# Moving a reciprocal, an attention product and gate injections between the steps of a fused recurrent kernel

## The chip, the cores and the metric

One core of a Trainium2 chip. The time is device time in microseconds (us) of one execution of the whole kernel, from a median of a few runs. A profile of one execution gives a span (first to last instruction) and a trace of every instruction with its start, its duration and what released it. Engines are called PE (TensorE; its weight loads are listed apart as PEld), DVE (VectorE), ACT (ScalarE), POOL (GpSimd) and SP (SyncE).

## The reference, cut to what matters

x is (2, 1024, 256): 2 sequences of 1024 time steps, width D = 256, and there is one condition vector for each sequence. Four residual layers follow one another; the first three work on each time step alone, the last is a recurrence over time.

```python
x = x + attention(x, cond)       # 2 keys only (a fixed one, and one from cond), 16 heads, then W_proj
x = x + experts(x, cond)         # shared gated unit + top 2 of 8 experts, gates s_i / (sum of the top 2 + 1e-9)
x = x + u(cond) @ W_u + x @ W_e  # condition and stream, added
# LSTM over the 1024 steps, h of width 256, 2 sequences:
z = x_t @ Wx + b + h @ Wh;  i, f, o, g = split(z)
c = sigmoid(f) * c + sigmoid(i) * tanh(g);  h = sigmoid(o) * tanh(c)
x = x + hs
```

## The kernel before, in words

The LSTM is a chain of T = 1024 dependent steps, so the kernel is one loop of BATCHES = 128 iterations of U = 8 steps (u = 0 to 7). In the gaps of these steps the engines make the first three layers for the batch of 8 time steps that comes next (NB = 16 rows, 8 steps x 2 sequences). Each engine runs its own loop in the order in which it is written, and the engines meet only in semaphores that count steps; `now` is the count that belongs to the step.

**One step.** PE waits for `hid` (the h of the step before) and runs `recur` (L881 to L888) for the gates f, g and i, then o: weight loads from the ring `h_ring`, matmuls with `wh_sb`, 64 records of each, all at line L885. Then DVE transposes f (L676), g and i (L678) and o (L684) in PSUM, ACT takes tanh of them (L510, L513, L516), DVE forms c with one scan (L686), ACT takes its tanh (L519), DVE writes h (L702) and signals `hid`. What DVE does besides stands at the head of a step (L655 to L674, ahead of its first transpose) or in the slot between the scan and h (L688 to L700). What PE does besides stands after the four `recur` of a step (L902 to L935).

**The side work of one batch, by step.**
- u = 0: PE multiplies the stream by `we_sb` (`stream_mm`), the condition (`cond_mm`) and the shared unit (`down_mm(0)`) into `partial_b`, in bank 7. `stream_made` is signalled after `stream_mm`.
- u = 1: DVE forms x + attention (`attended`, L587) from `attn_b` and `x_a`; PE makes the scores and the routing logits (L738 to L750); ACT takes tanh of the logits (`fall`, L467) and of the scores.
- From there POOL runs `gates` (L364 to L418), one chain of small operations on (128 x 8) or (128 x 64), which asks DVE for three reciprocals: `ratio` (L577, in the slot of u = 2), `s_all` (L581, slot of u = 3) and `inv` (L585, slot of u = 5), the inverse of `den_eps` (L400). After it come `pad` (L353), a copy of the layer's output, and `weigh` (L424, `hid_e`).
- u = 2: PE `down_mm(1)` and `(2)`; u = 3: PE `sum_mm` (L780) gives `x3_b` in bank 7; u = 4: DVE `layer3` copies it to `x3` (L604); u = 4 and 5: PE `up_mm` (L754); u = 5: ACT `unit_acts` (L471, L472); u = 6 slot and head of u = 7: DVE `hidden_a` (L593) and `hidden_s` (L598); head of u = 0: DVE `turn(0)`, the transpose of `hid_s` (L601).
- u = 6: PE `inject_fo` twice (L792): the x-part of f and of o for the next 8 steps is put into their banks. u = 7: PE `inject_gi` (L792, after waits for `padded_out` and `t_gi`) the same for i and g, and then `attend` (L742), attention's product for a later batch, into `attn_b` in bank 5.
- POOL, after the last h of a batch: `half_h` (L452), `y_sb` (L457) and `move` (L429); `h_read` after the first lets DVE overwrite the ring (waited for in the slot of u = 0, L690).

The injected f and o stand in their bank with an offset (`fo = (u + U - FO_AT - 1) % U * B`) since they are made one step ahead of the batch's end; i and g use `u * B`.

PE's loop is written `nc.Fori(..., head_slot={PE_ENGINE: 0})`: the loop's first instruction is loaded at slot 0 of a fetch block, and the code ahead jumps over the padding.

Of the kernel before, what the change touches and what calls it, by code (L numbers as in the profile page):

```python
# [11 lines left out]
P = 128  # L12
# [11 lines left out]
U = 8  # L24
# [17 lines left out]
FO_AT = 6  # L42
# [21 lines left out]
def cond_stack_kernel(nc, x, small, wkv, wq, wproj, up, we, down, wproj2, wu, wx, wh, bias_z, y):  # L64
    ctx = ExitStack()
    with ctx:
# [260 lines left out]
        def _(pool):  # L327
# [36 lines left out]
            def gates(count):  # L364
# [19 lines left out]
                pool.tensor_tensor(lead[:, :, :], rivals, own_sel, ALU.subtract).then_inc(gate_step, 1)  # L384
                pool.wait_ge(gate_step, 7)
# [76 lines left out]
        def _(act):  # L462
# [42 lines left out]
            with act.Fori(READY, READY + T, U) as t:  # L505
                for u in range(U):
                    now = act.snap(t + (u + 1))
                    fo = (u + U - FO_AT - 1) % U * B
                    act.wait_ge(t_f, now)
                    nc.scalar.activation(f_act[:, :].rearrange("p (c b) -> p c b", b=B),  # L510
                                         t_f_b[:, :, fo:fo + B], ACT.Tanh).then_inc(a_f, 1)
                    act.wait_ge(t_gi, now)
                    nc.scalar.activation(gi_out.rearrange("p g (c b) -> p g c b", b=B),  # L513
                                         t_gi_b[:, :, :, u * B:(u + 1) * B], ACT.Tanh).then_inc(terms_in, 1)
                    act.wait_ge(t_o, now)
                    nc.scalar.activation(o_act[:, :].rearrange("p (c b) -> p c b", b=B),  # L516
                                         t_o_b[:, :, fo:fo + B], ACT.Tanh)
# [13 lines left out]
        def _(dve):  # L531
# [55 lines left out]
            def attended(src):  # L587
                nc.vector.tensor_tensor(x1[:, :, :, 0:NB], attn_b.unsqueeze(2).to_broadcast([P, C, J, NB]),
                                        src.unsqueeze(2).to_broadcast([P, C, J, NB]), ALU.add).then_inc(x1_out, U)
# [6 lines left out]
            def hidden_s(count, up_to):  # L596
                dve.wait_ge(hid_a_out, count)
                nc.vector.tensor_tensor(hid_s[:, :], hid_a[:, :], units[:, P:2 * P], ALU.mult).then_inc(hid_s_out, up_to)  # L598
# [17 lines left out]
            attended(x_first[:, 0, :, :])  # L616
# [5 lines left out]
            hidden_s(U, U)  # L622
# [10 lines left out]
            attended(x_first[:, 1, :, :])  # L633
# [10 lines left out]
            hidden_s(2 * U, 2 * U)  # L644
            dve.wait_ge(x3_made, READY)
            layer3(READY)
            dve.wait_ge(w_in["wh"], 16)
# [6 lines left out]
            with dve.Fori(READY, READY + T, U) as t:  # L654
                for u in range(U):  # L655
                    now = dve.snap(t + (u + 1))
                    if u == 0:
                        dve.wait_ge(hid_s_out, now)
                        turn(0, hid_s[:, :], hid_st, U)
                    elif u == 1:  # L660
                        dve.wait_ge(x_ready, now)
                        dve.wait_ge(stream_made, now)
                        attended(x_a[:, :, :])
# [9 lines left out]
                    elif u == 7:  # L673
                        hidden_s(now, U)  # L674
# [22 lines left out]
                    elif u == 5:  # L697
                        invert_inv(now)
                    elif u == 6:
                        hidden_a(now)  # L700
                    dve.wait_ge(cell_tanh, now)
# [6 lines left out]
        def _(pe):  # L708
# [31 lines left out]
            def attend():  # L740
                for c in range(C):
                    last = nc.tensor.matmul(attn_b[:, c, :], value_w[:, c * P:(c + 1) * P], w1_own[:, :],  # L742
# [20 lines left out]
            def stream_mm(up_to):  # L763
                for c in range(C):
                    last = tile_mm(c, x1[:, c, 0, 0:NB], we_sb[:, c, :], True)
                last.then_inc(stream_made, up_to)
# [11 lines left out]
            def sum_mm(up_to):  # L778
# [3 lines left out]
                last.then_inc(x3_made, up_to)  # L782
# [14 lines left out]
            BEHIND = (FO_AT + 1) * B  # L797

            def inject_fo(z, g):
                return inject(z, g, NB, x3[:, :, BEHIND:BEHIND + NB], ones[:, 16:32], True)  # L800
# [21 lines left out]
            attend().then_inc(attn_made, 1)  # L822
# [9 lines left out]
            stream_mm(READY)  # L832
# [6 lines left out]
            pe.wait_ge(own_first, 2)  # L839
            pe.wait_ge(hid_s_out, U)  # L840
            attend().then_inc(attn_made, 1)
            pe.wait_ge(x1_out, 2 * U)
# [19 lines left out]
            pe.wait_ge(own_first, 3)  # L862
# [168 lines left out]
```

## Time and profile before

| | |
|---|---|
| time, median of 3 runs | 2413.18 us (2410.02 to 2414.47) |
| the profiled execution: its time | 2409.16 us |
| the profiled execution: its span | 2407.4 us |
| PE, PEld, DVE, ACT, POOL busy | 85%, 63%, 59%, 36%, 49% of the span |
| chain that ended last, by engine | PE 37%, POOL 22%, DVE 20%, issue 12%, ACT 9% |

Times of rows are us from the span's start. A row of the timeline gives start, duration, engine, line, operation, what is written and read, how many instructions are merged (x64), and in brackets the idle time of that engine just before and what released it. Matmuls are pipelined and their ends are modelled. "issue" is idle time for which the profile shows no releaser. A row of 64 weight loads at L885 is the `recur` of one step; the width of its weights (128x8 and so on) tells the step.

### The profile page before, as it was taken

To read this page: it belongs to the slowest core of one execution; us is meant where nothing else is said; L and a number is where in the kernel's file an instruction comes from. 1 tells how busy PE (TensorE), PEld (TensorE's weight loads), DVE (VectorE), ACT (ScalarE), POOL (GpSimd) and SP (SyncE) were. 2 spreads that over 40 slices of the span, in tenths; PEclk is the share of its full clock that TensorE was granted. 3 is DMA by queue.
4 is the path that set the end of the run, shared out by engine and by line. 5 is a ranking of instruction groups with operands and counts; after the bars stand their busy time and mean duration, and the time that the engine had idled before them with its cause. 6 is when DMAs were issued, how large, how long until landed. Compare 5 with 4: busy or idle time off the path is not lost.

```text
span 2407.4 us, 200920 instructions
## 1 busy us (share of the span) xinstructions
PE 2051.9 (85%) x86306; PEld 1505.9 (63%) x86306; DVE 1420.3 (59%) x7602; ACT 876.7 (36%) x4761; POOL 1169.1 (49%) x5082
## 2 busy tenths in 40 slices
PE   6888888888888888888888888888888888888888
PEld 4666666666666666666666666666666666666666
DVE  2565665566566556656655665665566566556655
ACT  1333333333333333333333333333333333333333
POOL 3445445444544554454455445445544544544454
PEclk8999999999999999999999999999999999999999
DMA  3000000000000000000000000000000000000000
GB/s 135 4 3 2 3 3 2 2 3 3 2 3 3 2 2 3 3 2 3 3 2 2 3 3 2 3 3 2 2 3 3 2 3 3 2 2 3 3 2 3
DMA packets 57581, 14.54 MB, mean 6 GB/s; under 512 B 56161, under 2 KB 56161, under 8 KB 57058
## 3 DMA queue, kind: packets, MB, share of 16 engines
q1 hardware_dynamic: 57570, 14.39, 2.6%
q8 instruction: 8, 0.13, 0.0%
q14 instruction: 3, 0.02, 0.0%
HBM read 12.26 MB, written 2.10 MB: 6 GB/s over the span
## 4 chain that ended last, share of the span: by engine, by line
PE 37%; POOL 22%; DVE 20%; issue 12%; ACT 9%; DVEq 0%; POOLq 0%; ACTq 0%
PE bank L885 28%; DVE bank L678 9%; ACT terms L513 5%; DVE bank L686 5%; PE bank L792 5%; DVE h_ring L702 4%; ACT bank L519 4%; PE bank L742 3%; POOL beats L386 2%; POOL ties L387 2%; POOL ties L389 2%; POOL beats L391 2%; POOL lead L384 2%; POOL beats L358 1%; POOL top L394 1%
## 5 line engine op out<-in xcount | busy, mean ns | idle before, releaser
L885 PEld LDWEIGHTS bank<-wh_sb,h_ring 128*4 128x4 f32 (+2 forms) x65536 | 922.9, 94 | 705.9 <-DVE h_ring L702 700.1
L885 PE MATMUL bank<-wh_sb,h_ring 128*4 128x64 f32 (+2 forms) x65536 | 1107.9, 219 | 296.8 <-DVE h_ring L702 229.7
L510 ACT ACTIVATE f_act<-bank 128x4 f32<-128x4 f32 x1024 | 177.3, 173 | 1026.0 <-DVE bank L676 1026.0
L676 DVE STREAM_TRANSPOSE bank<-bank 128x64 f32<-128x64 f32 x1024 | 271.6, 265 | 390.7 <-PE bank L885 390.7
L678 DVE STREAM_TRANSPOSE bank<-bank 128x64 f32<-128x64 f32 x1024 | 271.5, 265 | 186.1 <-PE bank L885 186.1
L513 ACT ACTIVATE terms<-bank 128x8 f32<-128x8 f32 x1024 | 189.5, 185 | 280.3 <-DVE bank L678 280.3
L372 POOL TENSOR_TENSOR num<-one,fall 128x8 f32<-128x8 f32 x130 | 26.0, 200 | 532.1 <-ACT fall L467 532.1
L754 PE MATMUL bank<-up_sb,x 128*32 128x512 f32 x2080 | 274.0, 599 | 0.7 <-ACT fall L467 0.7
L684 DVE STREAM_TRANSPOSE bank<-bank 128x64 f32<-128x64 f32 x1024 | 271.6, 265 | 0.1
L760 PE MATMUL bank<-down_e,hid_t 128*16 128x256 f32 x3096 | 266.6, 380 | 0.0
L702 DVE SCALAR_TENSOR_TENSOR h_ring<-o_act,bank 128x4 f32<-128x4 f32 x1024 | 161.0, 157 | 138.6 <-ACT bank L519 95.0
L686 DVE TENSOR_TENSOR_SCAN bank<-terms 128x16 f32<-128x16 f32 x1024 | 205.6, 201 | 27.8
L516 ACT ACTIVATE o_act<-bank 128x4 f32<-128x4 f32 x1024 | 177.3, 173 | 39.6 <-DVE bank L684 0.2
L519 ACT ACTIVATE bank<-bank 128x4 f32<-128x4 f32 x1024 | 161.8, 158 | 56.5
L792 PE MATMUL bank<-bias_sb,small_sb 128*16 128x64 f32 (+1 forms) x4128 | 159.2, 219 | 0.0
L681 DVE SCALAR_TENSOR_TENSOR terms<-f_act,bank 128x4 f32<-128x4 f32 x1024 | 152.6, 149 | 0.0
L760 PEld LDWEIGHTS bank<-down_e,hid_t 128*16 128x16 f32 x3096 | 100.9, 97 | 51.8
L792 PE MATMUL bank<-wx_sb,padded 128*32 128x64 f32 (+1 forms) x4128 | 99.0, 221 | 32.9 <-DVE bank L678 32.6
L378 POOL TENSOR_TENSOR num<-num 128x8 f32<-128x8 f32 x520 | 103.8, 200 | 40.8
L585 DVE RECIPROCAL inv<-den_eps 128x1 f32<-128x1 f32 x130 | 21.3, 164 | 158.6 <-POOL den_eps L400 158.6
L792 PE MATMUL bank<-wx_sb,x 128*16 128x64 f32 x4128 | 106.1, 220 | 8.1 <-POOL wx_sb L440 1.5
L792 PEld LDWEIGHTS bank<-wx_sb,padded 128*32 128x32 f32 (+1 forms) x4128 | 78.8, 103 | 53.2 <-issue 53.2
(133 smaller groups left out, 2654.2 us busy)
## 6 DMA issues: line engine op xcount, KB each, us to landing
x_a<-in_x SPq DMA_DIRECT2D x129, 16.0 KB, 1.7
x_s<-in_x SPq DMA_DIRECT2D x129, 16.0 KB, 1.7
up_sb<-in_up SPq DMA_DIRECT2D x1, 2048.0 KB, 8.7
out_y<-y_sb SPq DMA_DIRECT2D x128, 16.0 KB, 1.4
down_sb<-in_down SPq DMA_DIRECT2D x1, 1536.0 KB, 12.5
wx_sb<-in_wx SPq DMA_DIRECT2D x1, 1024.0 KB, 14.2
wh_sb<-in_wh SPq DMA_DIRECT2D x1, 1024.0 KB, 16.3
wkv_sb<-in_wkv SPq DMA_DIRECT2D x1, 512.0 KB, 3.9
```

The costliest lines, as they stand in the source:

```text
L510: nc.scalar.activation(f_act[:, :].rearrange("p (c b) -> p c b", b=B), t_f_b[:, :, fo:fo + B], ACT.Tanh).then_inc(a_f, 1)
L513: nc.scalar.activation(gi_out.rearrange("p g (c b) -> p g c b", b=B), t_gi_b[:, :, :, u * B:(u + 1) * B], ACT.Tanh).then_inc(terms_in, 1)
L519: nc.scalar.activation(c_tanh, cell_c, ACT.Tanh).then_inc(cell_tanh, 1)
L676: nc.vector.transpose(bank[3][:, 0:HC], z_f_b[:, 0:HC]).then_inc(t_f, 1)
L678: nc.vector.transpose(bank[4][:, 0:HC], z_gi_b[:, 0:HC]).then_inc(t_gi, 1)
L684: nc.vector.transpose(bank[3][:, HC:2 * HC], z_o_b[:, 0:HC]).then_inc(t_o, 1)
L686: nc.vector.tensor_tensor_scan(cell_all, factor, addend, 0.0, ALU.mult, ALU.add).then_inc(cell, 1)
L702: nc.vector.scalar_tensor_tensor(out=h_ring[:, u, :, WIN - B:WIN], in0=o_act[:, :].rearrange("p (c b) -> p c b", b=B), scalar=1.0, in1=c_t ...
L754: last = nc.tensor.matmul(units[32 * j:32 * (j + 1), :], x1[:, c, 0, :], up_sb[:, c, j, :], start=(c == 0), stop=(c == C - 1), skip_group_ ...
L760: return nc.tensor.matmul(partial_b[32 * j:32 * j + NB, :], lhs, rhs, start=first, stop=False, skip_group_check=True)
L792: last = nc.tensor.matmul(z[32 * j:32 * j + rows, 0:HC], src[:, c, :] if c < C else const, wx_v[:, c, g, j, :] if c < C else bias_v[:, g, ...
L885: last = nc.tensor.matmul(z[32 * j:32 * j + row + B, 0:HC], h_ring[:, prev, c, WIN - B - row:WIN], wh_v[:, c, g, j, :], start=False, stop= ...
```

## The change

- `invert_inv` (the reciprocal `inv`) goes from DVE's slot of u = 5 to the head of u = 7, behind `hidden_s`.
- DVE's `turn(0)` goes from the head of u = 0 to the slot of u = 7.
- PE's `inject_gi` goes from u = 7 to u = 6, and both `inject_fo` from u = 6 to u = 7; the offsets of the two pairs are exchanged.
- PE's `attend` goes from u = 7 to u = 3, behind `sum_mm`; its target moves from bank 5 to bank 7. `x3_made` is signalled behind it, `stream_made` behind `down_mm(0)`.
- POOL's `pad` goes from behind `gates` into it, behind `lead` (L384), and copies the rows with the offset.
- PE's loop has no `head_slot`.
- Ahead of the loops: waits and the two first `attend` change accordingly, and `turn(0)` runs once more.

```diff
-FO_AT = 6
+GI_AT = 6
-        attn_b = bank[5][:, 64:64 + C * NB].rearrange("p (c t) -> p c t", c=C)
+        attn_b = bank[7][:, D + C * NB:D + 2 * C * NB].rearrange("p (c t) -> p c t", c=C)
+        attn_first_b = bank[6][:, C * NB:2 * C * NB].rearrange("p (c t) -> p c t", c=C)
...
+            BEHIND = (GI_AT + 1) * B
             def pad(count):
                 pool.wait_ge(x3_out, count)
-                return pool.tensor_copy(padded[:, :, NB:2 * NB], x3[:, :, NB:2 * NB])
+                return pool.tensor_copy(padded[:, :, NB:2 * NB], x3[:, :, BEHIND:BEHIND + NB])
...
                 pool.tensor_tensor(lead[:, :, :], rivals, own_sel, ALU.subtract).then_inc(gate_step, 1)
+                if between:
+                    between()
                 pool.wait_ge(gate_step, 7)
...
-                gates(i * U + (READY + U))
-                pad(i * U + (READY + U)).then_inc(padded_out, U)
+                gates(i * U + (READY + U), lambda: pad(i * U + (READY + U)).then_inc(padded_out, U))
...
-                    if u == 0:
-                        dve.wait_ge(hid_s_out, now)
-                        turn(0, hid_s[:, :], hid_st, U)
-                    elif u == 1:
+                    if u == 1:
...
                     elif u == 7:
-                        hidden_s(now, U)
+                        hidden_s(now)
+                        invert_inv(now)
...
-                    elif u == 5:
-                        invert_inv(now)
                     elif u == 6:
                         hidden_a(now)
+                    elif u == 7:
+                        dve.wait_ge(hid_s_out, now)
+                        turn(0, hid_s[:, :], hid_st, U)
                     dve.wait_ge(cell_tanh, now)
...
-            with nc.Fori(READY, READY + T, U, engines=(PE_ENGINE,), head_slot={PE_ENGINE: 0}) as t:
+            with nc.Fori(READY, READY + T, U, engines=(PE_ENGINE,)) as t:
...
-                    recur(z_f_b, GF, fo, prev).then_inc(z_f, 1)
-                    recur(z_gi_b, GC, u * B, prev)
-                    recur(z_gi_b, GI, 16 + u * B, prev).then_inc(z_gi, 1)
-                    recur(z_o_b, GO, fo, prev).then_inc(z_o, 1)
+                    recur(z_f_b, GF, u * B, prev).then_inc(z_f, 1)
+                    recur(z_gi_b, GC, gi, prev)
+                    recur(z_gi_b, GI, 16 + gi, prev).then_inc(z_gi, 1)
+                    recur(z_o_b, GO, u * B, prev).then_inc(z_o, 1)
                     if u == 0:
                         pe.wait_ge(hid_st, now)
-                        stream_mm(U)
+                        stream_mm()
                         cond_mm()
-                        down_mm(0)
+                        down_mm(0).then_inc(stream_made, U)
...
                     elif u == 3:
                         pe.wait_ge(partial_out, now)
-                        sum_mm(U)
+                        sum_mm()
+                        pe.wait_ge(own_out, now)
+                        attend(attn_b).then_inc(x3_made, U)
...
                     elif u == 6:
+                        pe.wait_ge(padded_out, now)
+                        pe.wait_ge(t_gi, now)
+                        inject_gi()
+                    elif u == 7:
                         pe.wait_ge(t_f, now)
                         inject_fo(z_f_b, GF)
                         pe.wait_ge(t_o, now)
                         inject_fo(z_o_b, GO)
-                    elif u == 7:
-                        pe.wait_ge(padded_out, now)
-                        pe.wait_ge(t_gi, now)
-                        inject_gi()
-                        pe.wait_ge(own_out, now)
-                        attend()
```

## Rows read from the trace of the kernel before

**Rows 1.** The page, part 4: the chain that ended last, by engine.
```profile
PE 37%; POOL 22%; DVE 20%; issue 12%; ACT 9%; DVEq 0%; POOLq 0%; ACTq 0%
```

**Rows 2.** Timeline of one iteration, `recur` of u = 2, 4 to 7, 0, 1, 2.
```profile
1200.37 0.90 PEld L885 LDWEIGHTS bank<-wh_sb,h_ring 128*8 128x8 f32 x64 [0.23 <-DVE h_ring L702]
...
1204.53 0.91 PEld L885 LDWEIGHTS bank<-wh_sb,h_ring 128*12 128x12 f32 x64 [0.55 <-DVE h_ring L702]
...
1206.61 0.91 PEld L885 LDWEIGHTS bank<-wh_sb,h_ring 128*14 128x14 f32 x64 [1.05 <-DVE h_ring L702]
...
1209.70 0.91 PEld L885 LDWEIGHTS bank<-wh_sb,h_ring 128*16 128x16 f32 x64 [2.05 <-DVE h_ring L702]
...
1211.78 0.89 PEld L885 LDWEIGHTS bank<-wh_sb,h_ring 128*2 128x2 f32 x64 [0.25 <-DVE h_ring L702]
...
1214.46 0.89 PEld L885 LDWEIGHTS bank<-wh_sb,h_ring 128*4 128x4 f32 x64
...
1216.61 0.90 PEld L885 LDWEIGHTS bank<-wh_sb,h_ring 128*6 128x6 f32 x64 [0.71 <-DVE h_ring L702]
...
1218.69 0.90 PEld L885 LDWEIGHTS bank<-wh_sb,h_ring 128*8 128x8 f32 x64 [0.23 <-DVE h_ring L702]
```

**Rows 3.** Timeline of u = 5, and the waits: us in total, times, longest.
```profile
1209.10 0.22 POOL L400 TENSOR_SCALAR den_eps<-den 128x1 f32<-128x1 f32 x1 [0.16 <-POOL den L362]
...
1209.42 0.16 DVE L585 RECIPROCAL inv<-den_eps 128x1 f32<-128x1 f32 x1 [1.16 <-POOL den_eps L400]
...
DVE inv L585 <- POOL den_eps L400: 158.6, 130, 5.2
```

**Rows 4.** Timeline of u = 7: injection and attention's product.
```profile
1212.70 0.27 DVE L678 STREAM_TRANSPOSE bank<-bank 128x64 f32<-128x64 f32 x1 [0.18 <-PE bank L885]
...
1213.08 0.30 PEld L792 LDWEIGHTS bank<-wx_sb,padded 128*32 128x32 f32 x16 [0.41 <-issue]
...
1213.92 0.52 PEld L742 LDWEIGHTS bank<-w_own,value_w 128*128 128x128 f32 x4
```

**Rows 5.** Timeline of u = 6: the last weight loads of `inject_fo` for o.
```profile
1211.35 0.17 PEld L792 LDWEIGHTS bank<-bias_sb,small_sb 128*16 128x16 f32 x8
```

**Rows 6.** Timeline of u = 3 and the head of u = 4.
```profile
1203.46 0.52 PEld L780 LDWEIGHTS bank<-small_sb,partial 128*128 128x128 f32 x4
...
1204.51 0.19 DVE L604 COPY x<-bank 128x32 f32<-128x32 f32 x1
...
1205.01 0.27 DVE L676 STREAM_TRANSPOSE bank<-bank 128x64 f32<-128x64 f32 x1 [0.31 <-PE bank L885]
```

**Rows 7.** Timeline of DVE, head of u = 7.
```profile
1211.73 0.29 DVE L598 TENSOR_TENSOR hid_s<-hid_a,bank 128x128 f32<-128x128 f32 x1
```

**Rows 8.** Timeline of POOL: `lead`, the first operation behind `inv`, `weigh`, `half_h`.
```profile
1204.54 0.29 POOL L384 TENSOR_TENSOR lead<-sel 128x64 f32<-128x64 f32 x1
...
1210.29 0.20 POOL L411 TENSOR_TENSOR comb<-s_top,inv 128x8 f32<-128x8 f32 x1
...
1212.22 0.61 POOL L424 TENSOR_TENSOR hid_e<-gelu_act,gate_w 128x256 f32<-128x256 f32 x1
...
1213.94 0.24 POOL L452 TENSOR_TENSOR half_h<-h_ring,half 128x32 f32<-128x32 f32 x1 [1.11 <-DVE h_ring L702]
```

**Rows 9.** Timeline of DVE: a transpose in the slot of u = 1; h of u = 0.
```profile
1199.84 0.29 DVE L601 STREAM_TRANSPOSE hid_t<-hid_e 128x128 f32<-128x128 f32 x1
...
1216.40 0.16 DVE L702 SCALAR_TENSOR_TENSOR h_ring<-o_act,bank 128x4 f32<-128x4 f32 x1 [0.29 <-ACT bank L519]
```

**Rows 10.** Timeline of DVE: its first instruction after the loop's back edge.
```profile
1214.09 0.31 DVE L601 STREAM_TRANSPOSE hid_t<-hid_s 128x128 f32<-128x128 f32 x1 [0.29 <-issue]
```

**Rows 11.** Timeline of PE: first `recur` in the loop, and the same of pass two.
```profile
58.80 1.08 PE L885 MATMUL bank<-wh_sb,h_ring 128*4 128x64 f32 x64 [2.11 <-issue]
...
78.62 1.08 PE L885 MATMUL bank<-wh_sb,h_ring 128*4 128x64 f32 x64
```

**Rows 12.** The page, part 3: DMA of instructions, whole run: packets, MB, share.
```profile
q8 instruction: 8, 0.13, 0.0%
```

More of the change, by code:

```diff
@@ L615, in _ @@
             dve.wait_ge(attn_made, 1)
-            attended(x_first[:, 0, :, :])
+            attended(attn_first_b, x_first[:, 0, :, :])
             mask_first(1)
@@ L621, in _ @@
             hidden_a(U)
-            hidden_s(U, U)
+            hidden_s(U)
             dve.wait_ge(hid_s_out, U)
@@ L632, in _ @@
             dve.wait_ge(attn_made, 2)
-            attended(x_first[:, 1, :, :])
+            attended(attn_first_b, x_first[:, 1, :, :])
             mask_first(2)
@@ L738, in scores, with attend @@
                     nc.tensor.matmul(scores_b, score_w[:, c, :], x_s[:, c, :], start=(c == 0), stop=(c == C - 1))
-            def attend():
+            def attend(attn):
                 for c in range(C):
-                    last = nc.tensor.matmul(attn_b[:, c, :], value_w[:, c * P:(c + 1) * P], w1_own[:, :],
+                    last = nc.tensor.matmul(attn[:, c, :], value_w[:, c * P:(c + 1) * P], w1_own[:, :],
                                             start=True, stop=True)
@@ L761, in tile_mm, with stream_mm @@
                                         skip_group_check=True)
-            def stream_mm(up_to):
+            def stream_mm():
                 for c in range(C):
                     last = tile_mm(c, x1[:, c, 0, 0:NB], we_sb[:, c, :], True)
-                last.then_inc(stream_made, up_to)
+                return last
             def cond_mm():
@@ L776, in down_mm, with sum_mm @@
                 return last
-            def sum_mm(up_to):
+            def sum_mm():
                 for c in range(C):
@@ L781, in sum_mm @@
                                             start=True, stop=True)
[L782 removed]
+                return last
             wh_v = wh_sb[:, :, :].rearrange("p c (g j m) -> p c g j m", g=4, j=J)
@@ L821, in _ @@
             pe.wait_ge(own_first, 1)
-            attend().then_inc(attn_made, 1)
+            attend(attn_first_b).then_inc(attn_made, 1)
             pe.wait_ge(value_out, 3)
@@ L831, in _ @@
             pe.wait_ge(we_ident, C)
-            stream_mm(READY)
+            stream_mm().then_inc(stream_made, READY)
             pe.wait_ge(w_in["wproj2"], 16)
@@ L839, in _ @@
             pe.wait_ge(own_first, 2)
+            attend(attn_first_b).then_inc(attn_made, 1)
+            pe.wait_ge(x1_out, 2 * U)
             pe.wait_ge(hid_s_out, U)
-            attend().then_inc(attn_made, 1)
-            pe.wait_ge(x1_out, 2 * U)
             route()
@@ L872, in _ @@
             pe.wait_ge(partial_out, READY)
-            sum_mm(READY)
+            sum_mm().then_inc(x3_made, READY)
+            pe.wait_ge(own_first, 3)
+            pe.wait_ge(x3_out, READY)
+            attend(attn_b)
             pe.wait_ge(wx_scaled, 3)
-            pe.wait_ge(x3_out, READY)
             inject_fo(z_f_b, GF)
```

32 lines of the change are left out of this document (15 added, 17 removed).

## The prediction

> **What bounds the kernel now.** I read the chain of waits first. It belongs to no one engine: PE has 37%, and POOL has 22%, although POOL is busy only half of the time [rows 1]. So somewhere POOL's own chain is what the recurrence waits for. The timeline of one iteration says where. The start of `recur` in each step gives the length of the step before it [rows 2]: u = 2 and 3 take 4.16 us together, and u = 4, 6 and 1 (1216.61 to 1218.69) take 2.08 each. That is the bare recurrence, and nothing else in those steps reaches the end of one. Three steps are longer: u = 5 takes 1209.70 - 1206.61 = 3.09, u = 7 takes 1214.46 - 1211.78 = 2.68, u = 0 takes 1216.61 - 1214.46 = 2.15. The iteration is 1218.69 - 1200.37 = 18.32 us, and 128 of them are 2345 of the span's 2407.4 us.
>
> The 1.01 us of u = 5 is the reciprocal `inv`: it stands in DVE's slot ahead of h, POOL signals `den_eps` only at 1209.32, DVE has been idle 1.16 us by then, and h is queued behind it. This happens in each iteration (130 times, 158.6 us of idle time, of which some 0.2 us each would be idle anyway) [rows 3]. The 0.60 us of u = 7 is PE's: `inject_gi` can start only when g and i are transposed (1212.97), starts at 1213.08, and `attend` follows at 1213.92 and holds PE to 1214.46 [rows 4], while h would have let `recur` start at 1211.78 + 2.08 = 1213.86. That start of 1214.46 is the one `recur` in rows 2 that waited for nobody, which is the mark of a PE-bound step. The 0.07 us of u = 0 is in DVE: it is idle for 0.29 us ahead of h [rows 9], in the one slot where two waits stand ahead of h (for `h_read` and for the tanh). That pair of waits stays.
>
> **The change part by part,** per iteration.
>
> *The reciprocal, u = 5 to head of u = 7.* It frees the 1.01 us of u = 5. What is late next in u = 5? ACT's tanh of the unit and PE's `up_mm`, which already ran beside the waiting, end in time, since the same `up_mm` in u = 4 leaves that step at 2.08. At its new place DVE reaches it after `hidden_s`. On the new clock u = 6 starts at 1206.61 + 2.08 = 1208.69 and u = 7 at about 1210.83 (below), so the head of u = 7 begins at 1210.78 and `inv` at 1211.07. `den_eps` is there by 1209.32, or 1209.6 if POOL is pushed by the moved `pad` (0.21 of work, and its wait for `layer3`, below). Some 1.4 us are spare, so DVE doesn't wait. The head must hold 0.29 + 0.16 = 0.45 us [rows 3, 7]; `hidden_s` starts 0.05 ahead of `recur` (1211.73, 1211.78), and the f transpose comes 0.48 after it (1205.01 - 1204.53) [rows 2, 6, 7], so there are 0.53. Fits by 0.08, and the f transpose has a further 0.18 us of idle behind it [rows 4]. Cost 0; bounds 0 to 0.05.
>
> *Who waits for the late `inv`.* POOL: its `comb` ran at 1210.29 and now can't run before 1211.27, 0.98 us later. From `comb` to the end of `weigh` were 1212.83 - 1210.29 = 2.54 us [rows 8], less the `pad` that stood between them, so `weigh` ends at 1213.8 at the latest. Its first reader is DVE's transpose in the slot of u = 1, which comes after 1216. Behind `weigh` in POOL's queue is `half_h`, and that one has a tight reader: h of u = 0 waits for `h_read`. `half_h` would end at about 1213.8 + 0.1 + 0.24 = 1214.15. The new u = 0 starts at 1212.92 and writes h 1216.40 - 1214.46 = 1.94 later, at 1214.86 [rows 2, 9]. Spare: 0.7 us. Cost 0. `y_sb`, `move` and SP's store and loads are behind that and are next needed at u = 1 and u = 4. Cost 0.
>
> *Injections exchanged, `attend` gone from u = 7.* `inject_fo` in u = 6 cost nothing: its last weight load ended at 1211.35 + 0.17 = 1211.52, before the next `recur` at 1211.78 [rows 2, 5]. In u = 7 it has the same place in the step: 2.08. `inject_gi` alone, now in u = 6, still has the wait for the transpose: it lets the next instruction go 1213.92 - 1211.78 = 2.14 us after the step's start [rows 4], and `recur` is wanted at 2.08. Cost 0.06; bounds 0 and 0.13 (if PE must wait for what the matmuls' modelled ends show). So u = 7 gives back 0.60, u = 6 takes 0.06. Its wait for `padded_out` is nothing: the copy now ends near 1205.2.
>
> *`attend` behind `sum_mm` in u = 3.* `sum_mm` starts at 1203.46 [rows 6]; one such group of four wide weight loads holds PE 1214.46 - 1213.92 = 0.54 us [rows 2, 4]; two of them end at 1204.54, and `recur` of u = 4 is wanted at 1204.53. Cost 0.01; bounds 0 and 0.07 (one more wait on the way, by the 0.07 of u = 0). `layer3` now waits for both, so it runs at about 1204.65 to 1204.85 instead of 1204.51; the f transpose behind it on DVE is at 1205.01 [rows 6]. Cost 0. POOL's `pad` waits for `layer3`; `lead` ends at 1204.83 [rows 8], so it waits hardly at all, and the chain behind is about 0.3 us later, which is counted above. `stream_made` behind `down_mm(0)`: `attended` stands at the head of u = 1 and those products are done when h of u = 0 is. Cost 0.
>
> *`turn(0)` in the slot of u = 7.* The same kind of transpose, 0.29 us, stands in the slot of u = 1, and that step is 2.08 [rows 2, 9]. Cost 0. It leaves the head of u = 0, where nobody waited for it.
>
> *The loop head.* Two things. First, the back edge. PE's own doesn't show before, since `attend` lies over it. DVE's takes 0.29 us [rows 10]. After the change no `attend` covers PE's. What is left is the time from the end of the loads of `inject_fo`, 1211.52 - 1209.70 = 1.82 us after the step's start, to `recur` at 2.08 [rows 2, 5]: 0.26 us certainly, and more if PE's sequencer runs ahead while the o injection waits for its transpose. A back edge of DVE's size would stick out by 0.03 at the worst place. I take 0; bounds 0 and 0.2. The Trainium skill (Advanced Engine Details and Errata, Control Flow Timing) puts a compare-and-branch at about 108 ns; by that the edge is covered, and even bare it would add 14 us in all. DVE's row is nearly three times that figure.
>
> Second, fetching. The whole run moved 8 instruction packets [rows 12] for 128 passes, so the body isn't fetched again in each pass. In pass one it was: 78.62 - 58.80 = 19.82 us against 18.32, and 2.11 us of idle "issue" time stand ahead of the first `recur` [rows 11]. Once all is in place, steps of 2.08 stand all over the body, so running from one block into the next shows nowhere. So where the boundaries lie is worth nothing per pass. At the entry 0 to 2.1 us are saved once; I take 1.
>
> **Sum.** Per iteration 1.01 + 0.60 - 0.06 - 0.01 = 1.54 us, new iteration 16.78. 128 x 1.54 = 197 us, and 1 at the entry. Against the profiled execution's own time: 2409.2 - 198 = 2211. The median of the runs is 4.0 above that execution, so 2215 as a median.
>
> **The rivals.**
> *A: as summed.* 2215. With the unknown costs at their ends: 128 x (0.2 + 0.07 + 0.06) = 42 us more gives 2257, 128 x (0.06 + 0.01) = 9, the other 1 us at the entry and no offset of 4 for the median give about 2200.
> *B: PE's back edge lies bare,* 0.29 us as DVE's [rows 10]: 128 x 0.29 = 37, so 2252. For it: `attend` no longer lies over it. Against: the o injection's wait gives PE's queue time.
> *C: POOL's chain becomes the bound.* `inv` later by a second moves `weigh` and `half_h`, and h of u = 0 waits for `h_read`. I find 0.7 us spare. If that is out by 1.2 us, 0.5 sticks out: 64 us, 2279. Against: every term is from a row, and POOL idles 1.11 us before `half_h` [rows 8].
> *D: `attend` isn't hidden in u = 3* and its 0.54 us goes on the path: 128 x 0.53 = 68, 2283. This is also the case in which the change only moves one of its two stalls. Against: 1204.54 to 1204.53 above. The two numbers are close, so it is the part with the least cover.
> *E: slower. The unaligned body no longer stays loaded.* If each pass paid what pass one and its entry did, 1.50 + 2.11 = 3.61 us, the iteration is 20.39 and the time 2215 + 462 = 2677; it decides from 1.54 us per pass on. The page Runtime: NRT & Kernel Launch of the Trainium skill (Instruction fetch mechanics) says that a taken branch to a block outside the engine's instruction memory stalls on a fetch, and gives PE 2048 instructions in blocks of 256. By the row, 8 packets for 128 passes, the body stays; one block more because of the offset is what would have to tip it. The 8 x 64 loads and as many matmuls of `recur` in a pass [rows 2], and about a third as many besides by the code, are well under that page's figure, so by it too E needs bad luck.
>
> **How the numbers follow.** A 0.70, B 0.12, C 0.07, D 0.07, E 0.04. The predicted time is A's, 2215. The range takes A and B: 2200 to 2257, 0.82. A measurement of this kernel can tell about 0.2% (5 us) from no change. A to D are all faster by far; E is slower, unless only part of its price is paid. Faster 0.95, same 0.01, slower 0.04.
>
> **What would show it.** In the timeline after: starts of `recur` 2.08 apart for u = 1 to 5 and 7, 2.14 after u = 6, 2.15 after u = 0, and an iteration of 16.8. `inv` without a wait, at the head of u = 7; POOL waiting some 0.7 us for it ahead of `comb`. h as the releaser of `recur` in u = 0. POOL gone from the chain of waits. Wrong if: `recur` of u = 4 starts without a releaser 2.6 after u = 3 (D); h of u = 0 waits for POOL (C); u = 7 is 2.1 to 2.4 with "issue" ahead of u = 0 (B); many instruction packets (E).

## The result and the profile after

| | before | after |
|---|---|---|
| median, us | 2412.98 (4 runs, 2410.02 to 2414.47) | 2216.63 (4 runs, 2215.34 to 2218.07) |
| profiled execution: time, span | 2409.16, 2407.4 | 2216.50, 2214.7 |
| ratio | | 0.9188, 95% interval 0.9172 to 0.9204 |

The kernel is 8.1% faster. 2215 was forecast, with a range of 2200 to 2257.

The rows that answer to [rows 2], the starts of `recur` over one iteration of the changed kernel (`recur` is at L887 now), from u = 7 to the next u = 7:

```profile
1200.39 0.91 PEld L887 LDWEIGHTS bank<-wh_sb,h_ring 128*16 128x16 f32 x64
...
1202.48 0.89 PEld L887 LDWEIGHTS bank<-wh_sb,h_ring 128*2 128x2 f32 x64 [0.26 <-DVE h_ring L707]
...
1204.65 0.89 PEld L887 LDWEIGHTS bank<-wh_sb,h_ring 128*4 128x4 f32 x64 [0.73 <-DVE h_ring L707]
...
1206.73 0.89 PEld L887 LDWEIGHTS bank<-wh_sb,h_ring 128*6 128x6 f32 x64 [0.23 <-DVE h_ring L707]
...
1208.81 0.90 PEld L887 LDWEIGHTS bank<-wh_sb,h_ring 128*8 128x8 f32 x64 [0.63 <-DVE h_ring L707]
...
1210.89 0.90 PEld L887 LDWEIGHTS bank<-wh_sb,h_ring 128*10 128x10 f32 x64
...
1212.97 0.91 PEld L887 LDWEIGHTS bank<-wh_sb,h_ring 128*12 128x12 f32 x64 [1.05 <-DVE h_ring L707]
...
1215.10 0.91 PEld L887 LDWEIGHTS bank<-wh_sb,h_ring 128*14 128x14 f32 x64 [1.10 <-DVE h_ring L707]
...
1217.21 0.91 PEld L887 LDWEIGHTS bank<-wh_sb,h_ring 128*16 128x16 f32 x64
```

The iteration is 1217.21 - 1200.39 = 16.82 us, where it was 18.32. The start without a releaser that the `recur` of u = 0 had in [rows 2] is gone: at 1202.48 PE waits for h. The two places that have none now, u = 4 (1210.89, behind `attend`) and u = 7 (1200.39 and 1217.21, behind `inject_gi`), come on time or nearly so. Two steps are longer than forecast: u = 5 takes 2.13, where 2.08 was forecast, and u = 0 takes 2.17, where 2.15 was.

What answers to [rows 3], [rows 7] and [rows 8], from the timeline and from the list of waits (us in total, times, longest):

```profile
1200.55 0.16 DVE L589 RECIPROCAL inv<-den_eps 128x1 f32<-128x1 f32 x1
1200.79 0.20 POOL L416 TENSOR_TENSOR comb<-s_top,inv 128x8 f32<-128x8 f32 x1 [0.75 <-DVE inv L589]
1200.88 0.27 DVE L680 STREAM_TRANSPOSE bank<-bank 128x64 f32<-128x64 f32 x1 [0.17 <-PE bank L887]
...
1203.12 0.24 POOL L456 TENSOR_TENSOR half_h<-h_ring,half 128x32 f32<-128x32 f32 x1
...
1204.44 0.16 DVE L707 SCALAR_TENSOR_TENSOR h_ring<-o_act,bank 128x4 f32<-128x4 f32 x1 [0.29 <-ACT bank L523]
```
```profile
DVE inv L589 <- POOL den_eps L405: 10.5, 2, 5.3
```

DVE's wait for `den_eps` has fallen from 130 times, 158.6 us to 2 times, 10.5 us, both ahead of the loop. The wait has changed sides: POOL now waits for `inv`, 0.75 us. It can afford it: `half_h` ends at 1203.36 and h of u = 0 starts at 1204.44. The prediction named one sign more, that POOL leaves the chain of waits. The profile of the changed kernel doesn't follow that chain back into the loop, so this sign can't be read as it was named; in its list of waits, neither PE nor DVE waits more than twice for any one thing of POOL's. For the place of `attend` and `layer3`, compare [rows 4] and [rows 6]:

```profile
1209.82 0.52 PEld L785 LDWEIGHTS bank<-small_sb,partial 128*128 128x128 f32 x4
...
1210.26 0.53 PEld L747 LDWEIGHTS bank<-w_own,value_w 128*128 128x128 f32 x4
...
1211.02 0.19 DVE L608 COPY x<-bank 128x32 f32<-128x32 f32 x1 [0.19 <-PE bank L747]
```

`attend` follows `sum_mm` 0.44 us behind its start and is through at 1210.79, 0.10 before `recur` of u = 4; `layer3` waits 0.19 us for it and still ends 0.16 ahead of the f transpose.

For exact step lengths I took the distance between the ends of successive writes of h in the trace, the mean over all passes but the first two, in ns. A step is named by the h that ends it, so a late `recur` counts to the step that it starts.

| ends with h of u = | 0 | 1 | 2 | 3 | 4 | 5 | 6 | 7 | sum |
|---|---|---|---|---|---|---|---|---|---|
| before | 2761 | 2076 | 2080 | 2079 | 2083 | 3079 | 2092 | 2071 | 18320 |
| after | 2174 | 2075 | 2078 | 2079 | 2092 | 2130 | 2104 | 2086 | 16818 |

### The profile page after: what moved, and what is told of

It is laid out like the page before. It is cut to its first block and busy times, and to the rows that moved or that the text cites. A ratio compares the mean times of both kernels' runs of the same rounds, so it can differ in the third digit from the quotient of the medians.

```text
span 2214.7 us, 200920 instructions
## 1 busy us (share of the span) xinstructions
PE 2032.5 (92%) x86306; PEld 1496.1 (68%) x86306; DVE 1420.7 (64%) x7603; ACT 878.7 (40%) x4761; POOL 1178.9 (53%) x5082
## 5 line engine op out<-in xcount | busy, mean ns | idle before, releaser
L887 PEld LDWEIGHTS bank<-wh_sb,h_ring 128*2 128x2 f32 (+2 forms) x65536 | 922.4, 94 | 536.2 <-DVE h_ring L707 513.3
L887 PE MATMUL bank<-wh_sb,h_ring 128*2 128x64 f32 (+2 forms) x65536 | 1107.8, 219 | 122.7 <-DVE h_ring L707 56.4
L690 DVE TENSOR_TENSOR_SCAN bank<-terms 128x16 f32<-128x16 f32 x1024 | 218.3, 213 | 28.4
L378 POOL TENSOR_TENSOR num<-num,ratio 128x8 f32<-128x8 f32 x130 | 26.7, 205 | 163.7 <-DVE ratio L581 163.7
```

The source lines that it names most:

```text
L690: nc.vector.tensor_tensor_scan(cell_all, factor, addend, 0.0, ALU.mult, ALU.add).then_inc(cell, 1)
L887: last = nc.tensor.matmul(z[32 * j:32 * j + row + B, 0:HC], h_ring[:, prev, c, WIN - B - row:WIN], wh_v[:, c, g, j, :], start=False, stop= ...
```

## The experiments

All are timed beside runs of the kernel before on the same chip; its medians there were 2409.4 to 2411.2, and 2413.0 where the changed kernel was timed. So a difference between an experiment and the changed kernel's 2216.6 is uncertain by some 2 to 4 us; where it matters, the mean length of an iteration in the traces is the better measure (16.818 us in the changed kernel; 128 iterations). The edits are against the changed kernel unless it says otherwise.

**The reciprocal, by itself and with its companion.** First the kernel before with `invert_inv` late and `pad` early, nothing else:

```diff
                     elif u == 7:
                         hidden_s(now, U)
+                        invert_inv(now)
...
-                    elif u == 5:
-                        invert_inv(now)
...
-                gates(i * U + (READY + U))
-                pad(i * U + (READY + U)).then_inc(padded_out, U)
+                gates(i * U + (READY + U), lambda: pad(i * U + (READY + U)).then_inc(padded_out, U))
```

> The kernel before with two edits alone: the reciprocal inv at the head of u = 7, and pad inside gates. Theory: the stall of u = 5 was only the place of inv, 1.01 us a pass: 2413 - 128 x 1.01 = 2284 (2278 to 2295). Rival (POOL's chain is the bound wherever inv stands, since weigh and half_h come a second later): h of u = 0 waits for h_read and half of the gain or more is given back, 2340 or above.

Measured: 2284.93 us (2284.82 to 2286.6), ratio 0.9482 (0.9466 to 0.9498). The step that ends with h of u = 5 went from 3079 to 2083 ns, and the iteration from 18.320 to 17.333 us. The theory holds: 0.99 us a pass, where 1.01 was expected. Then the same without `pad`'s move:

> The kernel before with one edit: inv at the head of u = 7; pad stays behind gates. Theory: the edit needs pad's move. POOL reaches comb 1.0 us later while the steps come 1.0 us earlier, so pad ends near 1213.25 on the clock of rows 8 and inject_gi, wanted at 1212.07, waits 1.2 us for it, with attend behind: 2413 + 128 x (1.2 - 1.0) = 2439 (2415 to 2460). Rival: the stall of inv is a thing by itself and goes in any case: 2284.

Measured: 2419.02 us, ratio 1.0028 (1.0009 to 1.0048): no gain, but a small loss. High in its list of waits (us in total, times, longest) stands one that the lists of before and of the kernel above don't have:

```profile
PEld bank L791 <- POOL padded L353: 191.3, 128, 1.5
```

PE waits 1.49 us in each pass for `padded`. The step that ends with h of u = 5 is as short as above, the one that ends with h of u = 0 grew from 2761 to 3811 ns. So the late reciprocal hands its stall on, through POOL's queue, to whatever stands behind it there and has a reader; the move of `pad`, which looks like housekeeping, is what the whole gain hangs on: 2419 against 2285. The direction was right; the wait made the step 1.05 us longer, not 1.2.

**POOL's spare time** (the rival C). A number of small additions, chained, ahead of `half_h`:

```diff
+                for k in range(3):
+                    pool.wait_ge(gate_step, 30 + k)
+                    pool.tensor_tensor(idle[:, k, :], one[:, :], one[:, :], ALU.add).then_inc(gate_step, 1)
+                pool.wait_ge(gate_step, 33)
                 pool.wait_ge(hid, i * U + (READY + U + 1))
```

> The changed kernel with 3 more small additions in POOL's queue ahead of half_h, some 0.28 us each, 0.84 in all. Theory: in the changed kernel's trace half_h ends at 1203.36 and h of u = 0 starts at 1204.44, about 1.0 spare, so they cost nothing: 2217 within 6 us. Rival (POOL is already at the edge): 2217 + 0.84 x 128 = 2324, or a part of it.

Measured: 2215.82 us (two runs). With `range(6)`:

> The same with 6 more additions, 1.68 us. Theory: 1.0 of it is spare and h of u = 0 waits for the other 0.7 us: 2217 + 88 = 2305 (2290 to 2320). Rival: h_read is not what comes next behind PE and DVE, and it is still 2217.

Measured: 2343.96 us (two runs). The wait that C names is in the lists of both, first with 3 more, then with 6:

```profile
DVE h_ring L712 <- POOL half_h L461: 27.1, 92, 0.3
```
```profile
DVE h_ring L712 <- POOL half_h L461: 136.8, 127, 1.1
```

With 3, POOL is the last to release h in 92 passes, but DVE waits no longer than it does for ACT anyway (0.29 us each, 27.1 / 92); with 6 it waits 1.08. So C's mechanism is real, and the spare time is about what 3 additions take, some 0.8 us, where the forecast had 0.7. (With 3 the iteration is unchanged, 16.821 us, but not step by step: u = 4 is 0.08 us longer and u = 0, 5 and 6 together 0.08 shorter, by held scans: a scan of DVE's that POOL makes wait, see below.)

With 6 the step that ends with h of u = 0 grew by 0.76 us (2933 against 2174), close to the 0.7 expected. Another 0.25 us a pass is why 2344 lies above the expected range: in 24 of 126 passes TensorE's granted clock falls to half, 1.2 instead of 2.4 GHz, around the steps that end with h of u = 2 and u = 3. There these steps take 2.67 and 2.81 us in the mean, in the other passes 2.08. The stretch of the first of them in the loop, and the one behind it (columns: us, busy time of each engine, granted clock, DMA):

```profile
361.25:364.65 3.40, 3.40 (x92) 2.41 (x85) 1.33 (x9) 0.71 (x5) 1.27 (x7) 0.50 0.06 9
364.65:368.05 3.40, 3.39 (x144) 2.74 (x132) 2.18 (x13) 1.46 (x8) 1.73 (x8) 1.00 0.00 0
```

Two us earlier PE had waited for the late h of u = 0: its weight loads were idle for 1.50 us, against 0.73 in the changed kernel, whose clock stays at full speed through the loop. In the other passes the same wait had no such consequence, so the runs show that a longer wait can cost a second time, through the clock, and not when it does.

**Attention's product back in u = 7**, where it follows the injections of f and o:

```diff
                     elif u == 3:
                         pe.wait_ge(partial_out, now)
-                        sum_mm()
-                        pe.wait_ge(own_out, now)
-                        attend(attn_b).then_inc(x3_made, U)
+                        sum_mm().then_inc(x3_made, U)
...
                         inject_fo(z_o_b, GO)
+                        pe.wait_ge(own_out, now)
+                        attend(attn_b)
```

> The changed kernel with attention's product back in u = 7, behind the injections of f and o; its bank stays the new one. Theory: it starts some 1.86 us after the step's start and holds PE 0.54 us, so recur of u = 0 starts at 2.40 to 2.44 instead of 2.08: 0.34 x 128 = 43 us more, 2260 (2250 to 2270). Rival: PE's sequencer or queue sets the start of recur of u = 0 and the product would be hidden there too: within 5 us of 2217. Rival: the product wasn't free in u = 3 and the gain is less than 25 us.

Measured: 2254.82 us (2254.27 to 2257.82), 38 more. From its timeline, `attend` in u = 7 (which began at 1205.55) and the `recur` behind it:

```profile
1207.48 0.52 PEld L747 LDWEIGHTS bank<-w_own,value_w 128*128 128x128 f32 x4
1208.03 0.89 PEld L887 LDWEIGHTS bank<-wh_sb,h_ring 128*2 128x2 f32 x64
```

`recur` starts 2.48 us after u = 7 began, where 2.40 to 2.44 was expected; the step that ends with h of u = 0 grew by 0.365 us, or 47 us in all, and some 9 us came back in u = 5 and 6 (2130 to 2083 and 2104 to 2083 ns; held scans, below). In u = 3 the product is hidden, in u = 7 it isn't.

**The injections in their old steps**, with the old offsets (the edits of the diff for `GI_AT`, `gi`, `BEHIND` and u = 6 and 7 undone, all else kept):

> The changed kernel with the injections in their old steps (f and o in u = 6, i and g in u = 7) and with the old offsets. Theory (the sum): the wait for the transpose of g and i costs up to 0.06 us in whichever of the two steps it stands, so the exchange is worth nothing: 2217 within 5 us. Rival: with i and g in u = 7 the back edge follows the latest PE work of the step and lies bare, 0.1 to 0.3 us a pass: 2230 to 2255. Rival: the exchange is what took PE's stall away: 2217 + 0.55 x 128 = 2287.

Measured: 2244.58 us (2243.26 to 2244.94), 28 more. The sum had the exchange at nothing; the rival of the bare back edge is nearer. The timeline at the end of `inject_gi` in u = 7, and the next `recur`:

```profile
1200.35 0.20 PEld L796 LDWEIGHTS bank<-bias_sb,small_sb 128*16 128x16 f32 x8
...
1200.37 0.16 DVE L706 SCALAR_TENSOR_TENSOR h_ring<-o_act,bank 128x4 f32<-128x4 f32 x1
...
1200.75 0.33 PEld L888 LDWEIGHTS bank<-wh_sb,h_ring 128*4 128x4 f32 x23 [0.21 <-DVE h_ring L706]
```

Between the end of the loads and `recur` lie 0.20 us; in the changed kernel, with the same injection in u = 6, `recur` follows 0.04 us behind the last loads:

```profile
1200.15 0.20 PEld L797 LDWEIGHTS bank<-bias_sb,small_sb 128*16 128x16 f32 x8
```

(with `recur` at 1200.39, above). (The first row of `recur` says x23 only because the view ends at 1201.) DVE had written h by 1200.53, and `recur` usually starts 0.05 behind it, not 0.22, so it isn't h that `recur` is late for. The step that ends with h of u = 0 took 2313 ns against 2174, and the 2174 hold 27 ns of a held scan (below) that the 2313 don't. So the edge costs 0.14 us as it stands, and 0.17 with the scan set apart, where it has only `inject_gi` ahead of it. Why, is argued and not shown: PE's sequencer can't issue that injection's instructions before the transpose is there, so it comes to the edge with no work queued. That is 18 us of the 28; 13 net of what u = 6 and 7 gave back (2104 to 2084, 2086 to 2072 ns). The rest is a held scan in u = 4 (2092 to 2245 ns, 20 us), less 6 us in u = 5; more on it next.

**The loop head aligned again:**

```diff
-            with nc.Fori(READY, READY + T, U, engines=(PE_ENGINE,)) as t:
+            with nc.Fori(READY, READY + T, U, engines=(PE_ENGINE,), head_slot={PE_ENGINE: 0}) as t:
```

> The changed kernel with the loop head at slot 0 of a fetch block again. Theory (the sum): where the blocks lie costs nothing per pass; entering the loop costs 0 to 2.1 us once. So 2217 to 2219. Rival: running from block to block, or the back edge, depends on the offset in each pass; then the step that ends with h of u = 0 moves by 0.05 us or more and the time by 6 us or more, either way.

Measured: 2226.06 us (2224.91 to 2226.61): 9.4 more, which the sum did not foresee. Some 2.7 us of it lie in the entry and pass one (below), the rest, 0.053 us a pass, in the loop (16.871 against 16.818 us). But that time doesn't lie where the rival put it, at the edge. The step that ends with h of u = 0 was even shorter (2158 against 2174 ns), and so were those of u = 5 and 6 (2087 and 2083 against 2130 and 2104); the one with u = 4 took 2228 instead of 2092. Its timeline in u = 4, POOL's product of the ties and DVE's scan:

```profile
1201.50 0.32 POOL L394 TENSOR_TENSOR ties<-ties,small_sb 128x64 f32<-128x64 f32 x1
1201.51 0.37 DVE L690 TENSOR_TENSOR_SCAN bank<-terms 128x16 f32<-128x16 f32 x1
```

and the same pair in the changed kernel:

```profile
1212.33 0.36 POOL L394 TENSOR_TENSOR ties<-ties,small_sb 128x64 f32<-128x64 f32 x1
1212.33 0.20 DVE L690 TENSOR_TENSOR_SCAN bank<-terms 128x16 f32<-128x16 f32 x1
```

One of the two is always held: the scan takes 0.37 and the product 0.32, or the scan 0.20 and the product 0.36. Over the passes of both kernels these are the only two cases: product 320 to 325 ns with scan 361 to 373, where the product's start is stamped 5 to 13 ns ahead of the scan's; and product 362 to 366 with scan 199 or 200, where it is stamped 1 to 6 ns ahead. The stamps alone don't say who came first, since the product's is ahead in both cases; that the first has its inputs and the other waits is a reading. Where the product starts much earlier, the scan loses less, as in the kernel with `inv` late and `pad` early:

```profile
1215.38 0.32 POOL L391 TENSOR_TENSOR ties<-ties,small_sb 128x64 f32<-128x64 f32 x1
1215.54 0.22 DVE L688 TENSOR_TENSOR_SCAN bank<-terms 128x16 f32<-128x16 f32 x1
```

In six of the kernels here (the changed one, this one, the one just named, `attend` back, the injections back, 3 additions more) the product's lead plus what the scan lost over 200 ns comes to 173 to 181 ns in every pass where the scan is held, for leads of 5 to 168 ns. So the scan waits until about 175 ns behind the product's start, and not to its stamped end, 320 ns behind it. That gave a theory that has nothing to do with fetching, and an edit to test it: POOL waits for the scan, so that it can't come first.

```diff
+                if held is not None:
+                    pool.wait_ge(cell, held)
                 pool.wait_ge(gate_step, 9)
                 pool.tensor_tensor(ties[:, :, :], ties[:, :, :], before, ALU.mult).then_inc(gate_step, 1)
...
-                gates(i * U + (READY + U), lambda: pad(i * U + (READY + U)).then_inc(padded_out, U))
+                gates(i * U + (READY + U), lambda: pad(i * U + (READY + U)).then_inc(padded_out, U),
+                      i * U + (READY + 5))
```

With the aligned loop head:

> The kernel with the loop head at slot 0 of a fetch block, and the same wait of POOL for the scan of u = 4. Theory: what the aligned head lost per pass is the scan of u = 4, held 0.15 us in nearly every pass because POOL's product starts 10 ns ahead of it; with the wait that goes, step u = 4 falls from 2.228 to 2.08, and 2226 to 2226 - 0.15 x 128 = 2207 (2204 to 2213), which is within 4 us of the same kernel without the aligned head. Rival: the aligned head costs PE something in each pass and the scan is a bystander: still 2220 or more.

Measured: 2205.95 us (2204.89 to 2207.6), 20 less than the same kernel without the wait. Without the aligned head:

> The changed kernel with one wait more in POOL: its product for the ties (the line that starts with the scan of u = 4) waits for that scan's end. Theory (scan and POOL's two-input operations exclude each other, first come first served): in the changed kernel the scan of u = 4 wins nearly always (213 ns in the mean), so the step u = 4 gains 0.01 us only; POOL comes 0.25 later, inside its spare time, and its meetings in u = 5 and 6 (244 and 220 ns) change: 2216 + 0 to -9. Rival: POOL being later by 0.25 us is not free: 2217 + up to 32.

Measured: 2204.12 us (2202.54 to 2204.89). Once the meeting is decided, the aligned head makes 1.8 us, and the iterations differ by 0.018 us (16.733 and 16.715), about the scatter of the runs. The scans' group in the three kernels, the changed one, the one with the aligned head, and the changed one with POOL's wait (total us, mean ns), shows that this is what the loop lost and gained:

```profile
L690 DVE TENSOR_TENSOR_SCAN bank<-terms 128x16 f32<-128x16 f32 x1024 | 218.3, 213 | 28.4
```
```profile
L690 DVE TENSOR_TENSOR_SCAN bank<-terms 128x16 f32<-128x16 f32 x1024 | 225.6, 220 | 27.7
```
```profile
L693 DVE TENSOR_TENSOR_SCAN bank<-terms 128x16 f32<-128x16 f32 x1024 | 205.9, 201 | 27.7
```

The wait gained more than expected (12.5 us, and 0.103 us x 128 = 13 by the iterations, not 0 to 9): it also moved POOL out of the scans of u = 5 (244 to 199 ns) and u = 6 (220 to 200).

**Single waits.** In DVE's slot of u = 0 two waits stand ahead of h; PE has two ahead of `inject_gi`:

```diff
                         dve.wait_ge(h_read, now)
+                        nc.vector.memset(seen[:, :], 0.0)
...
                     elif u == 5:
+                        pe.wait_ge(padded_out, now)
                         up_mm(1).then_inc(up_made, U)
                     elif u == 6:
-                        pe.wait_ge(padded_out, now)
```

> The changed kernel with no instruction of the two tight places behind two waits: in DVE's slot of u = 0 a tiny memset takes the wait for h_read, and PE waits for padded_out ahead of up_mm(1) in u = 5. Theory: of two waits ahead of an instruction one is an instruction of its own, after which the next has still to be issued, 0.05 to 0.09 us where it comes last. The step that ends with h of u = 0 goes from 2.174 to 2.09, u = 7 from 2.086 to 2.07: 0.1 x 128 = 13 us less, 2204. Rival: the 0.07 belongs to the wait for POOL (h_read) or to the loop's edge, and nothing changes in that step. By either, where POOL's operations meet DVE's scan may shift by some 10 ns and change the time by up to 6 us.

Measured: a median of 2215.41 us, but the seven runs stand in two groups, 2197.28 and 2197.65, and five from 2214.61 to 2216.34. The gap of 18 us is 128 x 0.14, about the price of a held scan in u = 4, so the likely reading is that in the upper group that scan is held. This isn't shown: the only profiled execution is of the lower group, and in it the scan of u = 4 takes 199 ns in the mean. In the same execution the step that ends with h of u = 0 took 2104 ns instead of 2174, so the theory of the two waits holds there, at 0.07 us, while u = 7 is unchanged (2084 against 2086), so PE's pair of waits cost nothing. As a kernel it isn't shown to be faster than the changed one; with POOL's wait for the scan it is:

> Both mends in the changed kernel: single waits in u = 0 and u = 7, and POOL's product after the scan of u = 4. Theory: 13 us from the waits and up to 9 from the scans: 2196 to 2206, and less scatter from small shifts, since the meeting in u = 4 is decided by a wait. Rival: the gains don't add, because the POOL chain's phase against DVE changes with each: above 2210.

Measured: 2196.02 us (2193.97 to 2196.48), ratio to before 0.911 (0.9098 to 0.9123), 20.6 below the changed kernel. It is the best of all here. Iteration 16.650 us, h of u = 0 at 2090 ns, the scans at 202 ns. Its five runs lie within 2.5 us, in one group.

**A body that doesn't stay loaded** (the rival E, made on purpose): PE's loop over two batches a pass, with the same work.

```diff
-            with nc.Fori(READY, READY + T, U, engines=(PE_ENGINE,)) as t:
-                for u in range(U):
+            with nc.Fori(READY, READY + T, 2 * U, engines=(PE_ENGINE,)) as t:
+                for half_pass in range(2 * U):
+                    u = half_pass % U
...
-                    now = pe.snap(t + (u + 1))
+                    now = pe.snap(t + (half_pass + 1))
```

> The changed kernel with PE's loop written over two batches a pass, so that its body has twice the instructions and there are 64 back edges, not 128; the work is the same. Theory (the case E of the forecast, made on purpose): such a body no longer stays loaded and pays in each batch what pass one paid, 1.5 to 3.6 us: 2217 + 190 to 460, and hundreds of instruction packets. Rival: blocks are fetched ahead of their use and only the back edge counts: 2217, or up to 10 us less if the back edge costs something.

Measured: 2948.39 us (two runs, 2933.16 and 2963.63), 732 more. From its page, and from its list of waits:

```profile
q8 instruction: 768, 12.58, 1.7%
```
```profile
PEld bank L887 <- issue: 473.0, 412, 3.9
```

768 packets of instructions instead of 7, that is 12 in each of the 64 passes, and PE idle with no releaser for up to 3.9 us at a time. A body of 12 packets is fetched anew in each pass; one of half that size stays. A batch takes 22.7 us instead of 16.8: the first of a pass, behind the branch, some 26.1, the second 19.4. So 5.9 us a batch are lost, not 1.5 to 3.6, and the price isn't all the fetch's. In nearly every pass TensorE's granted clock falls to 0.50 (1.2 instead of 2.4 GHz) during the long stall behind the branch, here while PE is idle for 3.46 us up to 1227.75:

```profile
1226.20:1239.70 13.50, 10.66 (x246) 8.33 (x250) 4.20 (x23) 2.12 (x14) 1.29 (x7) 0.50 0.03 6
1239.70:1247.60 7.90, 7.19 (x297) 5.01 (x293) 4.72 (x26) 3.54 (x18) 5.07 (x23) 0.99 0.01 4
```

The mean clock of the execution is 0.899, where the changed kernel has 0.997, which makes some 600 us at the lower level. If PE's work had set the pace in all of them, that would be up to 300 of the 732 us, an estimate and an upper bound; no run separates the two. The changed kernel itself moved 7 packets, one fewer than before [rows 12].

## Why the prediction was right, point by point

- **`inv`.** Forecast 1.01 us a pass off u = 5, no wait at the new place. Alone with `pad` it gave 1.00 (3079 to 2083 ns). In the changed kernel the step is 2130: 0.045 of it is a held scan, a cost that wasn't in the sum.
- **Who waits for the late `inv`.** POOL forecast to wait 0.7 us, measured 0.75; spare ahead of `h_read` forecast 0.7, read as 1.08 in the trace of after, by the runs with more additions some 0.8. That `inv` was worth nothing without `pad`'s move is what the part on POOL's queue implied but did not say: it priced the order given, not the alternative.
- **PE's stall in u = 7.** Forecast 0.60, measured 2761 - 2174 = 0.587. `attend` back in u = 7 costs 0.365 and the injections back 0.139, each by itself; together 0.50, and the other 0.08 is not attributed.
- **`inject_gi` in u = 6.** Forecast 0.06, bounds 0 and 0.13. u = 7 grew by 0.015 only (2071 to 2086). Too dear by 0.045.
- **`attend` in u = 3.** Forecast 0.01. u = 4 grew by 0.009, which is no more than its scan grew (200 to 212 ns), so the product itself cost nothing. That its weight loads could start 0.44 us and not 0.54 behind `sum_mm`'s gave it 0.1 us more cover than I had counted, so D was further off than it looked.
- **`turn(0)`.** Forecast 0. It wasn't run by itself; the step of u = 7 is 2.09 us with it, 0.015 more than before, and that includes what `inject_gi` costs.
- **The exchange of the injections.** Forecast worthless for the back edge; it is worth 0.14 us a pass at u = 0, or 0.17 with the scan set apart. The step that failed is the reading of the edge: I asked whether it is covered after the change, found that it is, and did not ask what it would be without the exchange. The time was not touched by this, since it was the changed order that was priced.
- **The back edge.** Taken at 0. The step that ends with h of u = 0 is 2174, of which 2076 is bare, 0.07 the two waits that single waits take off, and 0.027 the scan of u = 0 (227 ns against 200). Nothing is left for the edge: A, not B.
- **The loop head.** No cost per pass, as forecast, once the scan's meeting is set apart. The `recur` of u = 0 in pass one and in pass two are 75.46 - 56.57 = 18.89 us apart, and 19.82 before [rows 11]. With 58.80 - 56.57 = 2.23 at the entry that is 3.16 us to the start of pass two. 1.5 of it is what any pass gains, so the entry and pass one gave some 1.7, where 1 was taken. The aligned head by itself starts the first `recur` later by 1.8 us (58.40 against 56.57), and by 1.0 in the pair with POOL's wait (57.89 against 56.92), within the 0 to 2.1 that was forecast. The rows of the first `recur` show that the stall, which I read as a fetch, moved and didn't go:

```profile
56.57 0.96 PE L887 MATMUL bank<-wh_sb,h_ring 128*2 128x64 f32 x55
58.75 0.33 PE L887 MATMUL bank<-wh_sb,h_ring 128*2 128x64 f32 x9 [1.22 <-issue]
```

- **The sum.** 1.54 us a pass forecast; 0.949 (u = 5) + 0.587 (u = 0) - 0.009 (u = 4) - 0.012 (u = 6) - 0.015 (u = 7) = 1.50 measured. A cost that I had too high (0.045 for `inject_gi`) cancels a part of one that I had not at all (held scans, 0.1 us a pass in u = 0, 4, 5 and 6). That leaves the sum 5 us too low: it said 2211 for the profiled execution, and 2216.5 was measured. What closed the gap is the 4.0 us that the prediction added to come from that execution to a median. The changed kernel has no such offset (2216.50 and 2216.63), so the closeness of 2215 to 2216.6 is luck; within 5 us is what the sum itself achieved. With the scan of u = 4 held in every pass, 0.15 us x 128 = 19 us more, it would have been 2236 before anything is given back elsewhere, still inside the range.

## What to carry to other kernels

Where something that an engine waits for is moved later, follow the queue behind it on the engine that feeds it: the stall reappears at the first thing there that has a reader, and the companion move that prevents it can be worth the whole change (here 2419 against 2285). In a chain that is bound by latency, a start that waited for nobody well after its input was there marks the step where an engine is full; here its work cost nothing in another step that had the same engine idle. When a stall is added or made longer, look at the granted clock behind it before pricing the stall alone. When an edit with no work in it, like an alignment, moves the time by a few microseconds, look for a pair of instructions of two engines that start together before believing in the edit; a wait that fixes their order costs less than the toss.

## What the hardware showed that I had not expected

DVE's scan reads both its inputs from SBUF, as POOL's product does, and one holds up the other: the scan takes 0.20 us alone and 0.37 when POOL is stamped 5 to 13 ns ahead, and POOL's product 0.32 or 0.365 in turn. A few ns decide about 0.15 us. In one kernel that may be decided for a whole execution (the two groups 18 us apart, of which only the lower was traced); with 3 additions more it changes from pass to pass (72 of 128 held). The Trainium skill says this on the page SBUF — State Buffer: a vector instruction with two SBUF inputs contends with a GpSimd instruction that reads SBUF (Who interferes with whom), and whichever starts first has the port pair for the whole instruction (SBUF: two separate sides). The trace agrees that the two exclude each other, but both are held for less than "the whole instruction": the scan for 175 ns from the start of a product stamped 320, at leads of 5 to 168 ns alike (214 ns in the kernel with `inv` late and `pad` early, not 360), and the product for 45 ns, not for the scan's 200. POOL's stamps are rough, so this is what they show and not how the ports work.

A second wait ahead of an instruction cost 0.07 us on DVE and nothing measurable on PE. And a loop body that PE can't keep costs 5.9 us for some 16.8 us of work, the lower clock behind the stalls included. The Trainium skill, page Runtime: NRT & Kernel Launch (Instruction fetch mechanics), says that a taken branch whose target lies outside the current two-page window stalls on a fetch. The trace agrees for the body of 12 packets. For the body of half that size it doesn't, if the window is two packets: that body was not fetched again in 128 passes (7 packets in all, of 16.4 KB each by the larger body's 12.58 MB in 768).
